# Edge gather of a graph layer: one-hots of nodes laid column by column, with tags written in twos

## What is computed

```python
q = (x[src] @ qW).reshape(e, 4, 24)
k = (x[dst] @ kW).reshape(e, 4, 24)
v = (x[dst] @ vW).reshape(e, 4, 24)
s = exp(clip(sum(q * k, -1), -10, 10))
w = s / (segment_sum(s, src)[src] + 1e-8)
res = segment_sum(w[:, :, None] * v, src)        # 6250 x 96
out = layernorm(x + x + res)
```

## Time and profile before

| | us |
|---|---|
| median of 3 launches | 1706.58 |
| lowest, highest | 1704.21, 1707.38 |
| span of the profiled execution | 1709.3 |
| second phase in it, first comparison to last addition | 865.0 to 1668.3 |

### The profile page before, as it was taken

The page is one execution under the profiler, slowest core; times in us unless marked ns, Lnnn a source line. Parts: engine busy times, 40 slices in busy tenths (PEclk is TensorE's granted clock), DMA queues, the critical chain, the costliest instruction groups (busy, mean ns, idle before and its releaser), DMA issues.

```text
span 1709.3 us, 56067 instructions
## 1 busy us (share of the span) xinstructions
PE 1482.0 (87%) x19964; PEld 1425.5 (83%) x19965; DVE 1469.3 (86%) x2980; ACT 1265.3 (74%) x1844; POOL 1016.7 (59%) x764
## 2 busy tenths in 40 slices
PE   4873988888888988888769999999999999999990
PEld 3652878888788878887759999999999999999990
DVE  6988998898988998898158999999999999999987
ACT  2341665565666666665559999999999999999984
POOL 6230776777777776777725555555555555555551
PEclk8566999999999999999979999999999999999995
DMA  5673899999999999999897777777777777777732
GB/s 155 225 276 132 312 370 337 336 346 366 348 352 343 341 367 339 357 339 344 333 302 257 238 238 241 244 238 239 239 243 242 237 240 240 243 239 237 240 113 56
DMA packets 159451, 465.03 MB, mean 272 GB/s; under 512 B 36994, under 2 KB 59266, under 8 KB 152244
## 3 DMA queue, kind: packets, MB, share of 16 engines
q1 hardware_dynamic: 123572, 301.16, 54.1%
q0 software_dynamic: 35840, 163.36, 23.9%
HBM read 271.21 MB, written 209.73 MB: 281 GB/s over the span
## 4 chain that ended last, share of the span: by engine, by line
PE 80%; DVE 8%; issue 6%; DMA 2%; SPq 2%; ACT 1%; POOL 0%; DVEq 0%; POOLq 0%; ACTq 0%
PE two_a L1131 14%; PE two_b L1131 13%; PE meta L1193 12%; PE sum_bank L1193 12%; PE two_a L1214 7%; PE two_b L1214 7%; PE one_d L1204 3%; PE one_c L1204 3%; PE meta L1149 2%; PE one_d L1160 2%; DMA work<-kv_table 1%; PE sum_bank L1113 1%; SPq L825 1%; DVE acc L1614 1%; DVE cols_work L1315 1%
## 5 line engine op out<-in xcount | busy, mean ns | idle before, releaser
L698 POOL TENSOR_TENSOR work<-work 128x768 f32<-128x768 f32 x236 | 450.8, 1910 | 357.4 <-ACT work L939 357.4
L635 POOL DMA_INDIRECT sorted_rows<-work x448 | 501.3, 1119 | 215.2 <-issue 215.2
L948 ACT ACTIVATE work<-work 128x1024 f32<-128x1024 bf16 x236 | 500.8, 2122 | 0.0
L1131 PE MATMUL two_a<-work 128*128 128x192 bf16 x2688 | 268.5, 251 | 86.8 <-issue 84.3
L903 ACT ACTIVATE work<-two_a 128x768 f32<-128x768 f32 x224 | 181.5, 810 | 187.0 <-PE two_a L1131 186.2
L1131 PEld LDWEIGHTS two_a<-work 128*128 128x128 f16 x2688 | 220.0, 100 | 107.5 <-issue 89.0
L1131 PE MATMUL two_b<-work 128*128 128x192 bf16 x2688 | 267.5, 251 | 0.0
L1193 PE MATMUL meta<-work 128*128 128x100 f32 x1888 | 236.1, 278 | 0.8 <-DVE acc L1548 0.8
L1193 PE MATMUL sum_bank<-work 128*128 128x100 f32 x1888 | 235.2, 278 | 0.0
L1579 DVE TENSOR_REDUCE work<-work 128x32 f32<-128x768 f32 x236 | 225.0, 953 | 8.2
L1131 PEld LDWEIGHTS two_b<-work 128*128 128x128 f16 x2688 | 225.9, 100 | 6.8
(11 more groups left out here) (229 smaller groups left out, 2211.8 us busy)
## 6 DMA issues: line engine op xcount, KB each, us to landing
work<-sorted_rows SPq DMA_DIRECT2D x472, 392.0 KB, 3.5
work<-sorted_local SPq DMA_DIRECT2D x56, 1024.0 KB
sorted_rows<-pad_rows SPq DMA_DIRECT2D x49, 392.0 KB, 4.5
work<-kv_table SPq DMA_DIRECT2D x112, 144.0 KB
sorted_rows<-work POOLq DMA_INDIRECT x448
kv_table<-work SPq DMA_DIRECT2D x12, 576.0 KB, 3.4
work<-in_x SPq DMA_DIRECT2D x12, 192.0 KB, 3.8
sorted_local<-work SPq DMA_DIRECT2D x56, 8.0 KB
```

What stands on the lines that cost most here:

```text
L635: pool.indirect_dma_start(out=rows_dram, out_offset=bass.IndirectOffsetOnAxis(ap=place_now[:, p, u, b:b + 1], axis=0), in_=payload[:, p, u ...
L698: pool.tensor_tensor(now[:, :, 0:D].rearrange("p c (h f) -> p c h f", h=HEADS), blk[:, k, :, :, D:2 * D].rearrange("p m c (h f) -> p (m c) ...
L948: act.activation(hot_f[:, k % HOTF], hot[:, k % HOTS].rearrange("p n c -> p c n"), ACT.Copy).then_inc(hotf_made[k % PSEM], 1)
L1131: mm = pe.matmul(to, picked[:, u % 2, k * P:(k + 1) * P], window[:, u, :, n, :], start=(n == 0), stop=(n == 2))
```

## The change

`hot` is now laid column by column: `[CH, P]`, 128 nodes side by side. `node1_row` holds the numbers 1 to 128 once and is read again for each column. ScalarE writes each tag twice side by side, so that the comparison, whose tag is the same along a whole column, reads its tag in pairs of neighbouring elements. The transposes and the cast to `hot_f` now read 128 neighbouring elements, where they read one in eight before. No instruction is added, removed or moved.

```diff
+TWIN = 2
-        node1_row = sb("node1_row", [P, P, CH], BF16)
+        node1_row = sb("node1_row", [P, P], BF16)
-        tags, at = share(at, [SBI, CH], BF16)
-        hot, at = share(at, [HOTS, P, CH], BF16)
+        tags, at = share(at, [SBI, CH, TWIN], BF16)
+        hot, at = share(at, [HOTS, CH, P], BF16)
...
-                    (node1_row[:], [[1, P], [0, CH]], 1, 0), (tile_row[:], [[1, NB], [0, HC]], 0, 0),
+                    (node1_row[:], [[1, P]], 1, 0), (tile_row[:], [[1, NB], [0, HC]], 0, 0),
...
-                        act.activation(tags[:, k, :].rearrange("p (m c) -> p m c", m=PAIR), blk[:, k, :, :, TAG],
-                                       ACT.Copy).then_inc(tag_made[k % PSEM], 1)
+                        act.activation(tags[:, k].rearrange("p (m c) i -> p m c i", m=PAIR),
+                                       blk[:, k, :, :, TAG].unsqueeze(3).to_broadcast([P, PAIR, BLK, TWIN]), ACT.Copy
+                                       ).then_inc(tag_made[k % PSEM], 1)
...
-                        act.activation(hot_f[:, k % HOTF], hot[:, k % HOTS].rearrange("p n c -> p c n"), ACT.Copy
+                        act.activation(hot_f[:, k % HOTF], hot[:, k % HOTS], ACT.Copy
...
-                            mm = pe.transpose(turned[k % 2][:, c, :], hot[:, k % HOTS, :, c], ident_b[:])
+                            mm = pe.transpose(turned[k % 2][:, c, :], hot[:, k % HOTS, c, :], ident_b[:])
...
-                        dve.tensor_tensor(hot[:, k % HOTS], tags[:, k, :].unsqueeze(1).to_broadcast([P, P, CH]),
-                                          node1_row[:], ALU.is_equal).then_inc(hot_made[k % PSEM], 1)
+                        dve.tensor_tensor(hot[:, k % HOTS].rearrange("p c (n i) -> p c n i", i=TWIN),
+                                          tags[:, k].unsqueeze(2).to_broadcast([P, CH, P // TWIN, TWIN]),
+                                          node1_row[:].rearrange("p (n i) -> p n i", i=TWIN).unsqueeze(1)
+                                          .to_broadcast([P, CH, P // TWIN, TWIN]), ALU.is_equal).then_inc(hot_made[k % PSEM], 1)
```

## The result

The changed kernel takes 1696.22 us (median of 6 runs, 1694.51 to 1701.78) against 1706.55 for the kernel before (6 runs, 1704.21 to 1710.68). The ratio on record is 0.9926, with a 95% interval of 0.9910 to 0.9943. The forecast was 12.6 us less. The medians differ by 10.3 us, the ratio gives 12.6 and its interval 9.7 to 15.4, so that the ratio meets the forecast to the tenth is luck. The profiled execution spans 1692.6 us, 16.7 less than the one before; the experiments put about 5 us of that down to a spread between executions and not to the change.

A forecast was written before the change was run, and what follows sets the result against it. The prediction took TensorE to bound the second phase. It subtracted 10.9 us for the transposes and 1.7 us for the iota, 12.6 in all, from 1706.6: 1694 us, range 1690 to 1700, wider range 1687 to 1703.

The forecast's parts named there:

- TensorE sets the pace: Second phase: TensorE has no wait in its 3.34 us a pair; VectorE follows 0.21 us behind, ScalarE also follows.
- The transposes: Second phase, 8 a pair: contiguous weight loads bring their distance from 62 to 56 ns, saving 0.048 us over 227 pairs, 10.9 us.
- Interpolating between 96 and 192 columns: Distance of transposes with 128 streamed columns, from matmuls 0.0423 and 0.082 us apart: 0.0555 us.
- The cast: ScalarE's cast to hot_f, 236 times: falls from 2123 ns to 1.04 us, worth nothing in time, being off the path.
- ScalarE's forecast wait for the transposes: Second phase: time freed by the shorter cast becomes waits for VectorE's clip and for the transposes before the copy L945.
- The early pairs' gain: First eight pairs: their gain is lost waiting for the ninth pair's transfer, ending at 891.27; only 227 pairs count.
- The comparison: VectorE's L1564, 236 times: reads the repeated tag in twos and still costs 686 ns, so 0.
- Its rival: Comparison L1564 falls to one element per clock, 1214 ns; VectorE needs 3.66 us a pair, time 1778 us; chance 0.06.
- The iota: Setup, node1_row: writes 128 elements instead of 1024, so VectorE's cast L1247 ends earlier; whole 1.7 us reaches the end.
- Rival 1: Transposes' 61 to 62 ns are set by turned output to PSUM, not the load; only the iota remains, 1704.9; chance 0.09.

The follow-up runs named there:

- e2: Changed kernel with ScalarE's cast to hot_f reading its elements 16 bytes apart again; 1697.29 us, ratio 0.9924 to the kernel before.
- e1: Changed kernel with the transposes loading elements 16 bytes apart again, the cast still contiguous; 1708.47 us, ratio 0.9990 to the kernel before.
- e4: Changed kernel with the long iota of 1024 elements put back beside the short one, its output unused; 1698.55 us, ratio 0.9931.
- e7: Changed kernel with GpSimd pausing its constants after the iotas until VectorE has cast both arrays of edges; 1696.64 us, ratio 0.9923.
- e5: Changed kernel with the transposes loading elements 4 bytes apart on even pairs and 8 bytes apart on odd pairs; 1698.55 us in one run.
- e3: Changed kernel with each tag written once and repeated along a whole column in the comparison; 1758.64 us in one run.

## Why the prediction was right

- **TensorE sets the pace.** Shown by e2: with ScalarE at 98% the time is that of the changed kernel. And by e1: 6 ns more on each transpose, and the period grows by eight times that. From 860 us on not "every slice" of the earlier trace rows is at 9 tenths: the one with the pause at the ninth pair has 6 and 5.
- **The transposes, 10.9 us.** Shown by e1. Load 148 to 98 ns (101 with the first of a row), distance 62 to 56 ns, period less 0.048 us, all as forecast. Over 227 pairs 0.0483 us is 11.0. From the ninth tag to the last addition the profiles differ by 10.0; against the kernel before, e2, e4 and e7 are 10.9 shorter and e5 12.5. That spread of 2.5 us is how TensorE comes out of the pause at the ninth pair. In all of them it resumes 1.4 us behind the ninth tag copy. After a marked wait of 3.39 us (the changed kernel) it takes 5.48 us to the next transposes, after 2.38 to 2.88 us (the kernel before, e2, e4, e7) 4.49 to 4.65, after 0.90 and 1.10 us (e1, e5) 3.02 to 3.09; the granted clock from 880 to 900 us was 0.83, 0.91 and 1.00. Like with like, the kernel before less e2 is 10.9, and e1 less e5 is 10.9.
- **Interpolating between 96 and 192 columns** gave 55.5 ns; 56 were measured. At what duration a load begins to space the transposes stays open between the 115 ns of e5, which fit, and the 148 of e1, which do not.
- **The cast, 1.04 us forecast, 1.049 measured, and worth nothing.** The tag copy with 16 elements takes 0.21 us in the timeline, with 8 it took 0.20. ScalarE's forecast wait for the transposes does not show: all of its idle time is in front of exp.
- **The early pairs' gain is swallowed.** Right: ScalarE's wait grew from 3.56 to 6.50 us. That a longer pause also costs clock afterwards, about 1 us against the kernel before, was not in the sum.
- **The comparison costs what it did.** 686 ns. The line that put it there was drawn through its own row and that of L1470, so that it lies on it says nothing; what spoke for it was that L1470, with runs of 2, took 0.60 ns an element over all. Its rival is real when the tag is single (e3), but its price was 20 us too high, since VectorE's need was taken as 3.13 us where it is 3.04: the overlap that a wait destroys was not counted.
- **The iota, 1.7 us.** The end of the cast moved by 1.71, as said; "I let the whole 1.7 us reach the end" was the weak step. 0.5 to 1.1 us of it reached the first phase, as far as the spread lets one see. This term is below what the times can tell. The page of the Trainium skill that the prediction names here, Advanced Engine Details and Errata, Mode Summary, says it only of those VectorE instructions that use both ports; e7 shows that GpSimd's work is what holds the cast (3.33 us beside the last iotas, 1.07 with GpSimd at rest), and no run shows by which port.
- **Rival 1** (turned output sets 62 ns) is refuted by the row of transposes at 56 ns.
- **Luck.** The main term came out to a tenth by its mechanism. That the total did as well is chance: the iota counted for less than its 1.7 us, the restart took back about 1 us in the profiled execution, and the time is known only within 9.7 to 15.4 us.

On the pages of the Trainium skill that disagreed: the strided load was the slower one (148 against 98 ns), as the 16-byte lines of SBUF — State Buffer, "Door 1: The DMA port swizzle", have it, against the reading of "packed or strided" in TensorE: Matmul & The Clock Gate, Weight-path perf modes, as equally fast. But e5 departs from the first page too, which gives full bandwidth from two hits on a line: at 8 bytes two elements share a line and the load still took 115 ns against 98.

## What to carry to other kernels

An engine at 98% may be a follower: ask whose output it waits for, and price an edit at zero unless the engine that waits for nothing gets shorter. What moves that engine can be as small as 6 ns per instruction, if it comes 8 times in each of 236 rounds; where weights are loaded with a stride, compare their load's duration with a contiguous one before anything else. Before you price a slower instruction on an engine that waits, look at what its instructions do when they need not wait: here the product started 0.08 us before the comparison in front of it had ended, so the slack was the idle time and that overlap. Neither the round less the idle time (3.13 us) nor the busy time is the need in general; an experiment that makes the engine the bound measures it.

## What was not expected of the hardware

- A weight load of 128 bf16 columns took 98 ns at a step of 2 and 4 bytes, 115 at 8 and 148 at 16 (medians), and only the last spaced the matmuls (62 instead of 56 ns).
- ScalarE's cast of 1024 bf16 elements took 1049 ns contiguous and 2090 to 2123 at 16 bytes: 1.02 to 1.05 ns more for each element.
- VectorE's cast of 1792 elements took 1.07 us with GpSimd at rest and 8.2 to 10.4 us beside an unbroken run of its constants, and ended 0.97 to 0.99 us after the last long one of them.
- A product on VectorE that had nothing to wait for started 0.084 us before the comparison in front of it had ended (e3); before the change it started 0.21 us behind it.
- The first phase of the same code differed by 7 us between executions. That is over half of the effect that was to be measured, and makes a comparison of two profiles' spans misleading where one of their stages is not.
